# Late tiles with one transpose and one zero-blocked product, a reordered start, and a last tile in halves

## The reference, cut to what matters

```
M_b  = f_b f_b^T / (128*16) + W          # f_b: (128, 16), one matrix for each batch
x    = x + gelu(x M_b^T + fc_bias + cond_b)
seg  = head (42), wrist (42), proprio (44 tokens)
logits_b = mean over segments of x, times gate_w ; scaled and shifted by silu(cond) time_w
w_be = top-2 of 4 softmax weights, renormed
x    = x + shared(x) + sum_e w_be * mask_e * (gelu(x ew1_e + eb1_e) ew2_e + eb2_e)
```

## Time and profile before

| what | before |
|---|---|
| median of 3 runs | 264.37 us (264.01 to 264.62) |
| the profiled execution | 262.98 us |
| its span, first to last instruction | 261.3 us |
| TensorE busy | 240.2 us (92%) |
| VectorE busy | 196.7 us (75%) |
| ScalarE busy | 145.0 us (55%) |
| granted TensorE clock, mean | 0.993 of 2.4 GHz |

### The profile page before, as it was taken

One profiled execution on the slowest core, in us unless ns is written; L12 is line 12 of the kernel. 1 busy time (PEld: TensorE's weight loads), 2 busy tenths in 40 slices (PEclk: granted clock), 3 DMA queues, 4 the chain that ended last, 5 costly groups with the idle time before them and its releaser, 6 DMA issues.

```text
span 261.3 us, 3479 instructions
## 1 busy us (share of the span) xinstructions
PE 240.2 (92%) x1230; PEld 200.7 (77%) x1230; DVE 196.7 (75%) x450; ACT 145.0 (55%) x270; POOL 15.1 (6%) x39
## 2 busy tenths in 40 slices
PE   8987788999899998999899998998989989999963
PEld 7875466888688877888678877886778879898852
DVE  0259899997689546977796966995799859679761
ACT  3478795353976089552966269544735175545500
POOL 6000000004000020002000020002000100010000
PEclk9999979999999999999999999999999999999999
DMA  6997000000000000100001000100000000100101
GB/s 129 219 292 144 1 0 3 0 0 0 3 21 19 0 3 1 40 3 0 0 1 43 0 0 1 43 0 0 0 17 25 0 0 14 29 0 1 40 3 40
DMA packets 17100, 7.41 MB, mean 28 GB/s; under 512 B 5523, under 2 KB 16443, under 8 KB 17083
## 3 DMA queue, kind: packets, MB, share of 16 engines
q1 hardware_dynamic: 16069, 6.98, 10.8%
q10 hardware_dynamic: 854, 0.18, 0.3%
q0 software_dynamic: 160, 0.02, 0.1%
HBM read 5.09 MB, written 2.10 MB: 28 GB/s over the span
## 4 chain that ended last, share of the span: by engine, by line
PE 67%; ACT 14%; DVE 14%; issue 3%; DVEq 0%; POOL 0%; ACTq 0%; POOLq 0%
PE ps L456 20%; PE ps L458 18%; PE ps L457 18%; ACT h L380 5%; PE ps L503 3%; DVE hs_lo L716 3%; ACT hs_hi L383 3%; DVE hs_lo L705 2%; ACT L380 2%; DVE hs_hi L711 2%; PE ps L473 2%; PE ps L462 2%; PE ps L487 2%; ACT L361 1%; PE ps L569 1%
## 5 line engine op out<-in xcount | busy, mean ns | idle before, releaser
L380 ACT ACTIVATE h<-ps,b_col 128x512 f32<-128x512 f32 (+1 forms) x160 | 92.4, 642 | 64.1 <-PE ps L458 49.4
L716 DVE SCALAR_TENSOR_TENSOR hs_lo<-h,w_be,hs_hi 128x512 fp32r<-128x512 f32 (+1 forms) x128 | 76.2, 656 | 0.0
L456 PE MATMUL ps<-x_hi,W_hi 128*128 128x512 f32 (+1 forms) x160 | 64.3, 402 | 8.2 <-ACT hs_hi L383 4.9
L456 PE MATMUL ps<-hs_hi,W_hi 128*128 128x512 f32 (+1 forms) x160 | 59.2, 370 | 5.2 <-DVE hs_lo L716 2.5
L457 PE MATMUL ps<-x_hi,W_lo 128*128 128x512 f32 (+1 forms) x160 | 59.1, 369 | 0.0
L458 PE MATMUL ps<-x_lo,W_hi 128*128 128x512 f32 (+1 forms) x160 | 59.0, 369 | 0.0
L458 PE MATMUL ps<-hs_lo,W_hi 128*128 128x512 f32 (+1 forms) x160 | 58.5, 365 | 0.0
L457 PE MATMUL ps<-hs_hi,W_lo 128*128 128x512 f32 (+1 forms) x160 | 58.2, 363 | 0.0
L711 DVE TENSOR_SCALAR hs_hi<-h,w_be 128x512 fp32r<-128x512 f32 (+1 forms) x128 | 48.2, 440 | 12.7 <-PE ps L458 6.7
L456 PEld LDWEIGHTS ps<-x_hi,W_hi 128*128 128x128 f32 x160 | 30.4, 190 | 20.4 <-ACT hs_hi L383 10.9
L456 PEld LDWEIGHTS ps<-hs_hi,W_hi 128*128 128x128 f32 x160 | 30.1, 188 | 10.9 <-DVE hs_lo L716 2.8
(11 more groups left out here) (106 smaller groups left out, 175.4 us busy)
## 6 DMA issues: line engine op xcount, KB each, us to landing
W_raw<-in_L_cond_ew SPq DMA_DIRECT2D x8, 256.0 KB, 5.5
out<-x_tok SPq DMA_DIRECT2D x8, 256.0 KB, 2.3
x_tok<-in_x SPq DMA_DIRECT2D x6, 168.0 KB
x_tok<-in_x SPq DMA_DIRECT2D x3, 176.0 KB
W_raw<-in_L_cond_sw SPq DMA_DIRECT2D x2, 256.0 KB, 4.6
x_tok<-in_x SPq DMA_DIRECT2D x3, 84.0 KB
F_raw<-in_fside_Bx1x1024x SPq DMA_DIRECT2D x3, 64.0 KB, 4.7
x_tok<-in_x SPq DMA_DIRECT2D x2, 88.0 KB
```

The costliest lines, as they stand in the source:

```text
L380: ins = nc.scalar.activation(span(h[:, k % 3, c, :], s), up_bank(k, c), ACT.Gelu_apprx_tanh, bias=b1_col[:, s, c:c + 1])
L456: nc.tensor.matmul(dst, w_hi, m_hi, start=start, stop=False)
L716: nc.vector.scalar_tensor_tensor(hs_lo[:, k % 2, :, c], h[:, k % 3, :, c], w_be[:, t * NB + b, s - 1:s], f32(hs_hi[:, k % 2, :, c]), ALU.m ...
```

## The change

1. **fside in padded form.** `F_pad` has 32 columns for each batch, 16 of data and 16 that GpSimd zeroes for the late tiles. A late tile takes one 128x128 transpose for its four batches. ScalarE then makes five copies instead of one: the whole 128x128 as weights (`fT_all`), and four blocks of 32 rows x 128 columns on the diagonal of `fT_block`, which GpSimd zeroes once, after the low part of the third weight. One fp32 product of 128 rows and 512 columns takes the place of four products of 16 rows. xT and the product wait for all five copies.
2. **The start reordered.** On the sync queue the first weight goes behind the five small loads for b1 and the gate. On VectorE time_gate comes before the segment sums, which become one call for four tiles; x1_low of tiles 2 and 3 goes behind split(0) and split(1). On ScalarE x1_high of tiles 2 and 3 and the high parts of the third and fourth weights go behind gelu(0) and gelu(1).
3. **Gates split in two.** The late groups read their logits at place 4 (`read_logits`) and rank them at place 5 (`gate_ranks`), which is behind out_sum.
4. **The last tile in halves.** split and down of the last step, the last out_sum, transposes, copies and the store go by two batches, with a PSUM bank for each half.

```diff
-        F_raw = sb("F_raw", [128, B, R])
+        RP = 128 // NB
+        F_pad = sb("F_pad", [128, B, RP])
+        fT_all = sb("fT_all", [128, 128])
-        fT_late = W1_raw[0:R, 1, :].rearrange("p (b d) -> p b d", d=D)
+        fT_block = W1_raw[:, 1, :].rearrange("p (b d) -> p b d", d=D)
...
-            load_weight(WEIGHTS[0])
...
+            load_weight(WEIGHTS[0])
             load_weight(WEIGHTS[1])
...
+            nc.gpsimd.memset(F_pad[:, NA * NB:, R:RP], 0.0).then_inc(pad_zero_ok, 1)
             pool.dma_start(cond_raw[:, :], cond).then_inc(cond_in, 16)
...
+            pool.wait_ge(w_lo_ok, made(2))
+            nc.gpsimd.memset(fT_block, 0.0).then_inc(block_zero_ok, 1)
...
             def fT_late_copy(t):
                 act.wait_ge(fT_ps, t + 1)
-                act.wait_ge(w_lo_ok, made(2))
+                act.wait_ge(block_zero_ok, 1)
                 act.wait_ge(M_ps, t)
-                nc.scalar.activation(fT_late, psLate[0:R, :].rearrange("p (b d) -> p b d", d=D), ACT.Copy
-                                     ).then_inc(fT_ok, 1)
+                nc.scalar.activation(fT_all[:, :], psLate[:, 0:128], ACT.Copy).then_inc(fT_late_ok, 1)
+                for b in range(NB):
+                    rows = slice(b * RP, (b + 1) * RP)
+                    nc.scalar.activation(fT_block[rows, b, :], psLate[rows, 0:128], ACT.Copy).then_inc(fT_late_ok, 1)
...
-                if t >= 1:
+                if t in (1, 2):
                     x1_high(t - 1)
                 if t >= 2:
                     weight_high(WEIGHTS[t - 2])
-            x1_high(NA - 1)
-            weight_high(WEIGHTS[2])
-            weight_high(WEIGHTS[3])
             act.wait_ge(b1_ok, 1)
             gelu(0)
+            for n in WEIGHTS[2:4]:
+                weight_high(n)
+            x1_high(NA - 2)
+            gelu(1)
             gate_tanh(0)
-            gelu(1)
+            x1_high(NA - 1)
...
+                if t >= NA:
+                    pe.wait_ge(pad_zero_ok, 1)
+                    nc.tensor.transpose(psLate[:, 0:128], F_pad[:, t * NB:(t + 1) * NB, :], ident[:, :]
+                                        ).then_inc(fT_ps, 1)
+                    return
...
+                if t >= NA:
+                    pe.wait_ge(fT_late_ok, (NB + 1) * (t - NA + 1))
+                    pe.wait_ge(xT_ok, t + 1)
+                    nc.tensor.matmul(psLate.rearrange("p (b d) -> p b d", d=D), fT_all[:, :], fT_block, start=True,
+                                     stop=True).then_inc(M_ps, 1)
+                    return
...
+                if k == K - 1:
+                    for b in range(0, NB, 2):
+                        pe.wait_ge(lo_ok, parts_until(k - 1) + b + 2)
+                        half = slice(b * L, (b + 2) * L)
+                        for c in range(CH):
+                            last = product3(psY[t % 2][:, half], W2_hi[:, s, c, :], W2_lo[:, s, c, :],
+                                            hs_hi[:, k % 2, c, half], hs_lo[:, k % 2, c, half], False,
+                                            b > 0 and c == CH - 1)
+                    last.then_inc(down_ok, 1)
+                    return
...
+            t = NT - 1
+            for half in range(2):
+                pe.wait_ge(outT_ok, NSEG * (t + 1 + half))
...
                 if t == 2:
                     output_rows()
                     weight_low(WEIGHTS[0])
-                    segment_sums(0, 2)
-            segment_sums(2, 4)
-            time_gate()
+                    time_gate()
+            segment_sums(0, 4)
             gate_in(0)
-            x1_low(NA - 1)
             dve.wait_ge(bias_in, 16 * 3)
             modulation()
             weight_low(WEIGHTS[1])
             weight_low(WEIGHTS[2])
-            gate_logits(0)
+            read_logits(0)
+            gate_ranks(0)
             split(0)
             gate_weights(0)
             weight_low(WEIGHTS[3])
+            x1_low(NA - 2)
             split(1)
+            x1_low(NA - 1)
...
                 g = late_gate(k, 4)
                 if g is not None:
-                    gate_logits(g)
+                    read_logits(g)
+                g = late_gate(k, 5)
+                if g is not None:
+                    gate_ranks(g)
...
-            out_sum(NT - 1)
+            last_sum(0)
+            last_sum(1)
```

More of the change, by code:

```diff
@@ L177, in build @@
         psOut = ps[:, 7, :]
+        psLast = [psOut, ps[:, RING[0], :]]
         block = ctx.enter_context(nc.Block())
@@ L274, in _ @@
                 load_x(c)
-            for t in range(NT):
+            for t in range(NT - 1):
                 sp.wait_ge(out_tok_ok, t + 1)
@@ L278, in _ @@
                              ).then_inc(out_left, 16)
-            sp.wait_ge(out_left, 16 * NT)
+            for half in range(2):
+                b = (NT - 1) * NB + half * NB // 2
+                sp.wait_ge(out_tok_ok, NT + half)
+                sp.dma_start(out[b:b + NB // 2, :, :].rearrange("b l d -> l b d"),
+                             x_tok[:, NT - 1, half * NB // 2:(half + 1) * NB // 2, :]).then_inc(out_left, 16)
+            sp.wait_ge(out_left, 16 * (NT + 1))
         @block.gpsimd
@@ L450, in _ @@
                     gate_tanh(g)
-            out_copy(NT - 1)
+            for half in range(2):
+                b = slice(half * NB // 2, (half + 1) * NB // 2)
+                act.wait_ge(out_ps, NT + half)
+                nc.scalar.activation(x_tok[:, NT - 1, b, :], psLast[half].rearrange("p (b d) -> p b d", d=D)[:, b, :],
+                                     ACT.Copy).then_inc(out_tok_ok, 1)
         @block.tensor
@@ L640, in _ @@
                     out_transpose(t)
-            out_transpose(NT - 1)
+            t = NT - 1
+            for half in range(2):
+                pe.wait_ge(outT_ok, NSEG * (t + 1 + half))
+                if half == 0:
+                    pe.wait_ge(out_tok_ok, t)
+                else:
+                    pe.wait_ge(h_ok, CH * K)
+                for b in range(half * NB // 2, (half + 1) * NB // 2):
+                    last = nc.tensor.transpose(psLast[half][:, b * D:(b + 1) * D], outT[:, t % 2, b * L:(b + 1) * L],
+                                               ident[:, :])
+                last.then_inc(out_ps, 1)
         @block.vector
@@ L708, in split @@
                 before_k = sum(NB for j in range(k) if STEPS[j][1] > 0)
-                for b in range(NB):
-                    c = slice(b * L + a, b * L + z)
-                    nc.vector.tensor_scalar(hs_hi[:, k % 2, :, c], h[:, k % 3, :, c],
-                                            w_be[:, t * NB + b, s - 1:s], None, ALU.mult).then_inc(hi_ok, 1)
-                for b in range(NB):
-                    c = slice(b * L + a, b * L + z)
-                    dve.wait_ge(hi_ok, before_k + b + 1)
-                    nc.vector.scalar_tensor_tensor(hs_lo[:, k % 2, :, c], h[:, k % 3, :, c],
-                                                   w_be[:, t * NB + b, s - 1:s], f32(hs_hi[:, k % 2, :, c]),
-                                                   ALU.mult, ALU.subtract).then_inc(lo_ok, 1)
+                group = NB // 2 if k == K - 1 else NB
@@ new lines, in split @@
+                for first in range(0, NB, group):
+                    for b in range(first, first + group):
+                        c = slice(b * L + a, b * L + z)
+                        nc.vector.tensor_scalar(hs_hi[:, k % 2, :, c], h[:, k % 3, :, c],
+                                                w_be[:, t * NB + b, s - 1:s], None, ALU.mult).then_inc(hi_ok, 1)
+                    for b in range(first, first + group):
+                        c = slice(b * L + a, b * L + z)
+                        dve.wait_ge(hi_ok, before_k + b + 1)
+                        nc.vector.scalar_tensor_tensor(hs_lo[:, k % 2, :, c], h[:, k % 3, :, c],
+                                                       w_be[:, t * NB + b, s - 1:s], f32(hs_hi[:, k % 2, :, c]),
+                                                       ALU.mult, ALU.subtract).then_inc(lo_ok, 1)
@@ new lines, in last_sum @@
+            def last_sum(half):
+                t = NT - 1
+                b = slice(half * NB // 2, (half + 1) * NB // 2)
+                dst_v, sum_v, x1_v = (ap.rearrange("p (b l) -> p b l", l=L)
+                                      for ap in (outT[:, t % 2, :], psY[t % 2], x1[:, t, :]))
+                if half == 0:
+                    dve.wait_ge(down_ok, AT[t, NS - 1] + 1)
+                    dve.wait_ge(x1b_ok, NSEG * NT)
+                    dve.wait_ge(out_ps, t - 1)
+                for at, dst, n in SEGS:
+                    nc.vector.tensor_tensor(dst_v[:, b, dst:dst + n], sum_v[:, b, at:at + n], x1_v[:, b, at:at + n],
+                                            ALU.add).then_inc(outT_ok, 1)
@@ L778, in gate_in, with read_logits @@
                                         AX.X, ALU.add).then_inc(gate_fold_ok, 1)
-            def gate_logits(g):
+            def read_logits(g):
```

(4 more changed lines are left out.)

26 lines of the change are left out of this document (13 added, 13 removed).

## The result

The changed kernel takes 256.38 us (median of 4 runs, 255.94 to 256.66), the kernel before 264.19 us in the same comparison (4 runs, 263.11 to 264.62). The ratio is 0.9702, 95% interval 0.9669 to 0.9735: 7.8 us faster, where I had forecast 5.5 and a time of 258.9 us.

What follows compares the result with a forecast made beforehand. VectorE bounds about 21 to 49 us, TensorE mostly until 249, then a serial chain. Start 0.3, transposes 1.0, products 0.6, gates 2.0, end 1.6 sum to 5.5; 264.37 - 5.5 = 258.9 us, range 257.5 to 261.0.

Steps and rivals of the forecast that it cites:

- start: Up to down(2): the new order gains only VectorE's gaps, chiefly before the logits; +0.3 us (0 to 0.6).
- late transposes and products: Late tiles: one transpose replacing four saves 1.0 us, one wide product replacing four saves 0.6 us.
- gates: Two downs waiting for the output sum: ranks moved behind it remove the stall; 2.0 us (1.2 to 2.0).
- end: Last tile: halves let TensorE start down earlier and shorten the work behind it; 1.6 us (1.0 to 2.4).
- The offset of the median: Whole time: the runs' median lies 1.39 us above the profiled execution, so the gain was subtracted from 264.37 us.
- The late products: Four late tiles: two instructions of 512 columns instead of eight of 128 save 0.15 us each, 0.6 us (0 to 1.1).
- The transposes: Late tiles 5, 6, 7: one transpose instead of four saves 0.33 us each, 1.0 us (0.8 to 1.1).
- six sums in a row: Last tile on VectorE: six half-size sums take longer than three, costing some 0.2 us more.
- It is ready some 0.4 us before VectorE asks: Start: the third weight's high part, now behind gelu(0), is ready some 0.4 us before VectorE asks.
- The rival of VectorE: VectorE takes over gains at the start, tile 4 and the second gate stall; 260.0 us, chance 0.15.
- The rival of the clock in the start: TensorE's clock falls through down(1) after two idle stretches, losing 1.4 us; 260.3 us, chance 0.08.
- more than I count: Fast wide products (+0.5), store with halved landing (+0.8), start worth 0.5; 257.4 us, chance 0.15.

Runs made afterwards that it cites:

- e1: Only the reordered start, put into the kernel before: 264.18 us against 264.38, ratio 1.0005.
- e2: Only the padded fside, one transpose and wide product of the late tiles, put into the kernel before: 262.34 us, ratio 0.9932.
- e3: Only the late groups' ranks moved behind the output sum, in the kernel before: 261.85 us, ratio 0.991.
- e4: Only the last tile in halves, put into the kernel before: 261.12 us, ratio 0.9891.
- e6: The whole change without the last tile in halves: 259.2 us, ratio 0.9811 against the kernel before.
- e5: The kernel before with ten added, unread TensorE products in the wait before the last down: 263.06 us against 264.15, ratio 0.9966.
- e7: The whole change with the late product cut into four of 128 columns, weights still 128 rows: 256.25 us, ratio 0.9707 against the kernel before.
- e10: The whole change with the last tile stored by one 256 KB transfer instead of two halves: 256.51 us, ratio 0.9729 against the kernel before.
- e9: The kernel before with three more semaphores that nobody uses: 263.76 us against 263.27, ratio 1.0006.

## Why the prediction came out wrong

| term | forecast | in the span | by its experiment |
|---|---|---|---|
| start | 0.3 | -0.1 (0.35 at full clock) | 0.2, within the noise (e1) |
| late transposes and products | 1.6 | 2.5 | 2.0 (e2) |
| gates | 2.0 | 2.3 | 2.5 (e3) |
| end | 1.6 | 2.1 | 3.3 (e4), 2.8 (e6) |
| outside the span | 0 | -0.5 | in e2 |
| sum | 5.5 | 6.8 - 0.5 = 6.3 | 8.0 |

The mechanisms were right in kind, and so was the direction. Two steps failed outright, the offset most of all, and the start failed in part.

**The offset of the median.** The step "The median of the runs is 1.39 above the profiled one, so I forecast 264.37 - 5.5 = 258.9" carries the difference over unchanged. It isn't a property of the measurement but, for the most part, a cost inside the kernel: by the times of the runs, the clock falls in the last down in over half of the executions, 1.4 us. The wait of 2.55 us was before my eyes, and I priced only the work behind it. The halves make two waits of 0.42 and 0.43 of it, and none of the seven profiles with a halved end shows a fall within the last down. Measured against profiled executions the change gives 262.98 - 256.66 = 6.3 us, 0.8 more than forecast; the median of before lies 1.2 us above its profiled execution, that of after 0.3 below: 6.3 + 1.2 + 0.3 = 7.8. So about 1.7 us of the 2.5 us by which the forecast missed is this step, 0.8 the sizes of the terms. Of the 1.7, some 1.2 to 1.4 are the fall in the last down; the 0.3 on the side of after are of the size of the wait in the start (0.51 us) which its profiled execution had and others need not have had. e5 shows the cause by itself: 1.1 us without any part of the change. I had a rival in which the clock falls, but only in the start, and only as a loss; that a change could end a fall was on no list.

**The late products**, "4 x 0.15 = 0.6 us (0 to 1.1)", measured 4 x 0.42 = 1.7 us. I had priced them by their instructions; e7 shows that their number costs nothing, and the rows of the weight loads put 0.40 us at the edges to weights of 16 rows. The transposes were near: 0.28 each against 0.33.

**Gates**, 2.0 against 2.3 in the span (0.65 and 1.68). The chain of reasons held, no new wait came up behind the ranks. The size was short since the idle time of a row understates a stall.

**The end**, 1.6 against 2.1 in the span. From down to the first sum the profile gained 3.07 - 1.72 = 1.35 us; the 1.3 for narrower matmuls was right. From there on I had 0.35 and the profile has 0.72: I had counted six sums in a row as a loss of 0.2, but the transposes wait only for the first three and start 0.61 us behind the sums' start instead of 0.88, and the copy 0.48 behind the transposes instead of 0.69. The two copies in a row cost 0.17 more than the one (from the copy to the end of the span 3.51 us in e10, 261.3 - 257.96 = 3.34 before), and the halved store gives 0.3 to 0.4 in the profiles instead of 0.1. The 0.15 us that I had as worked out by the Trainium skill (DMA: Bandwidth & Descriptors, Anatomy of one DMA) was a slip: the page has about 2.0 us and bytes over 436 GB/s, which makes 0.3 us for 128 KB less, an estimate by that page, and its figures are for GpSimd's queue, where this store goes by the sync queue. The rows of 1.9 and 2.3 us say 0.4, and the measurement decides.

**The start**, 0.3 against nothing in the two profiles. "It is ready some 0.4 us before VectorE asks" held where the clock held: in e7 and e10 VectorE did not wait for the high part of the third weight, and the start gained 0.35 us. It failed in the profiled execution, with the wait of 0.51 us, because it took for granted that up(0) comes at its old time. The same stretch, by windows as in the earlier trace rows, first before, then after, then e7:

```profile
18.90:22.70 3.80, 3.44 (x24) 3.15 (x25) 3.36 (x13) 3.49 (x10) 0.00 (x0) 1.00 1.02 197
```
```profile
18.90:22.70 3.80, 3.80 (x20) 3.80 (x21) 3.36 (x16) 2.97 (x9) 0.00 (x0) 0.56 1.04 173
```
```profile
18.90:22.70 3.80, 3.50 (x25) 3.17 (x25) 3.31 (x16) 2.91 (x9) 0.00 (x0) 1.00 1.02 171
```

At a granted clock of 0.56, mostly the lower level, the twelve products of ones in front of up(0) took 2.68 us instead of 1.50, up(0) came about 1 us later (22.74 against 21.73), gelu(0) with it, and the weight, which now stands behind gelu(0), too. That the new order let such a fall reach VectorE is what the layout missed. GpSimd's memset took 0.53 us (forecast 0.4) at 29.96, and cost nothing that can be seen: VectorE's short logit instructions beside it took 0.22 us, as before. The rival of VectorE took this one gain over, and no other. The rival of the clock in the start named another fall, behind the two idle stretches: it came too (0.57 from 36 to 40 us) and cost nothing, since down(2) waits for VectorE. Of the rivals, "more than I count" (257.4) came nearest, for another reason than it gave.

## What to carry to other kernels

- Look at every run of the kernel before starting from its profile: where the times fall into two groups, find what differs, and ask whether the change touches it. Don't add the distance between median and profiled execution as a constant.
- A wait of TensorE in front of the last serial stage costs its idle time and, in some executions, half the clock in what follows. Cutting the producer's work so that TensorE starts on a part pays twice; cutting below the width at which the pace stops to follow it (here 256 columns) loses again.
- Price a stall between the starts of neighbouring matmuls that would follow each other, not by its idle time, and look at the row of weight loads where the shape of the weights changes.
- When work is moved behind an instruction, ask what happens if that instruction comes a microsecond late, and compare several profiles before naming a cause: here two profiles differed by a fall of the clock as well as by the change.

## What the runs showed of the hardware

- After 2.5 us without a matmul the granted clock fell to the lower level (0.50) in three profiles, with the first matmul behind the gap (e3) or 1.3 us later (e1, e2), and did not in the last down of three others (before, e6, e9). The times of the runs suggest it for 37 of 66 executions of the kernel before, 1.4 us each.
- Ten products whose result nobody reads, put in that gap, made the kernel before 1.1 us faster (e5).
- From 18.90 to 22.70 us the granted clock was 0.55 to 0.60 in seven of fourteen profiles and 1.00 in the other seven, in old and new starts alike.
- A small product between large ones took 0.25 us more in front and 0.15 us more to the next load when its weights had 16 rows than when they had 128, zeros included (e7 against before).
- High and low matmuls of 128 and of 256 columns start every 0.111 and 0.118 us, of 512 every 0.23.
